# A mixed four-stage transformer block on one core: products over the full array that nothing reads, in the first stretch of the heads stage

## What is computed

```python
x = L0_attn_embedding                              # (4, 1024, 128)
x = _layernorm(x + _L0_attn_ref(x, Wq, bq, ...))   # 16 heads of 8
x = _layernorm(x + _L0_ffn_ref(x, ...))            # 2 layers of local attention and a gated ffn
x = _layernorm(x + _L1_attn_ref(x, ...))           # rotary positions, Taylor softmax
x = _layernorm(x + _L1_ffn_ref(x, ...))

# _L0_attn_ref
q, k, v = split_heads(e @ Wq + bq), split_heads(e @ Wk + bk), split_heads(e @ Wv + bv)
scores = jnp.einsum('bhqd,bhkd->bhqk', q, k) * scale
attn = jax.nn.softmax(scores, axis=-1)
av = jnp.einsum('bhqk,bhkd->bhqd', attn, v)
out = av.transpose(0, 2, 1, 3).reshape(b, s, e) @ Wo + bo
```

## Time and profile before

| | us |
|---|---|
| median of 3 runs | 1731.61 |
| the runs | 1735.49, 1728.04, 1731.61 |
| the profiled execution, its own time | 1729.86 |
| span of its trace | 1728.1 |

### The profile page before, as it was taken

How to read it: one execution, slowest core, us unless ns; L and a number is a source line. 1 busy time by engine, 2 the same in 40 slices (tenths; PEclk the granted TensorE clock), 3 DMA queues, 4 the chain that set the end, 5 groups by cost and what they waited for, 6 DMA issues and landing times. The chain is left out here.

```text
span 1728.1 us, 41224 instructions
## 1 busy us (share of the span) xinstructions
PE 1574.9 (91%) x14986; PEld 806.7 (47%) x14986; DVE 1393.2 (81%) x2949; ACT 1187.2 (69%) x2461; POOL 787.9 (46%) x605
## 2 busy tenths in 40 slices
PE   6499999999999999968999998999999989699887
PEld 4122223223223232244777775667777755344454
DVE  6799999999999999646999996689999968343355
ACT  5168888888888888865788784267888744555421
POOL 4211111112221114247888882288888825644301
PEclk9589999999999999988999999999999999999999
DMA  5203111000000000111223222322232222000001
GB/s 166 75 20 129 34 36 38 20 20 20 21 20 20 21 22 17 49 51 39 59 57 83 61 54 62 80 53 62 57 92 62 55 57 66 1 1 2 1 18 32
DMA packets 124384, 79.14 MB, mean 46 GB/s; under 512 B 50594, under 2 KB 110940, under 8 KB 123932
## 3 DMA queue, kind: packets, MB, share of 16 engines
q1 hardware_dynamic: 122796, 75.44, 16.4%
q10 hardware_dynamic: 1392, 1.12, 0.2%
HBM read 42.82 MB, written 16.79 MB: 34 GB/s over the span
## 5 line engine op out<-in xcount | busy, mean ns | idle before, releaser
L1101 DVE TENSOR_REDUCE hd_top<-hd_pX 128x1 f32<-128x512 f32 x1024 | 623.6, 680 | 32.8 <-PE hd_pX L935 32.8
L1069 ACT ACTIVATE hd_E<-hd_pS 128x1024 f32<-128x1024 f32 x512 | 524.7, 1025 | 82.1 <-PE hd_pS L951 59.9
L935 PE MATMUL hd_pX<-l_K,l_Q 48*128 48x512 bf16 x1024 | 342.3, 396 | 26.1 <-DMA l_Q<-q_parts 21.5
L968 PE MATMUL hd_pO<-hd_E,l_V 128*32 128x256 f32 x4096 | 327.6, 392 | 18.0 <-ACT hd_O L1044 18.0
L951 PE MATMUL hd_pS<-l_Q,l_K 50*128 50x512 bf16 x1024 | 310.5, 384 | 3.0 <-DMA l_Q<-hd_negp 2.0
L883 POOL TENSOR_TENSOR hd_inv<-hd_OS,hd_minus 128x16 f32<-128x16 f32 x31 | 90.0, 2902 | 443.4 <-ACT hd_OS L1057 430.8
L1815 POOL TENSOR_TENSOR w_inv<-w_ss,w_mhalf 128x16 f32<-128x16 f32 x64 | 186.4, 2913 | 0.0
L1710 ACT ACTIVATE w_pS<-w_pS,w_nb 128x128 f32<-128x128 f32 x512 | 178.5, 365 | 6.5 <-DVE w_nb L1901 4.7
L1804 POOL TENSOR_TENSOR w_C<-w_C,w_N 128x1024 f32<-128x1024 f32 x64 | 151.0, 2360 | 61.3 <-DVE w_N L1875 61.0
L968 PEld LDWEIGHTS hd_pO<-hd_E,l_V 128*32 128x32 f32 x4096 | 81.7, 108 | 171.3 <-issue 124.7
L951 PEld LDWEIGHTS hd_pS<-l_Q,l_K 50*128 50x128 bf16 x1024 | 59.0, 94 | 197.8 <-issue 184.7
(11 more groups left out here) (290 smaller groups left out, 2785.0 us busy)
## 6 DMA issues: line engine op xcount, KB each, us to landing
w_VA<-w_V SPq DMA_DIRECT2D x127, 128.0 KB, 2.3
l_Q<-q_parts SPq DMA_DIRECT2D x192, 32.0 KB
l_K<-k_parts SPq DMA_DIRECT2D x168, 32.0 KB
m<-early_rows SPq DMA_DIRECT2D x64, 64.0 KB, 1.7
f_H<-m SPq DMA_DIRECT2D x32, 128.0 KB, 2.7
f_X<-m SPq DMA_DIRECT2D x16, 256.0 KB, 3.0
q_parts<-pj_ptq SPq DMA_DIRECT2D x8, 384.0 KB, 2.5
k_parts<-pj_ptk SPq DMA_DIRECT2D x8, 384.0 KB, 2.5
```

The source lines that it names most:

```text
L935: nc.tensor.matmul(px[:, :], Q[m.j][rows, m.z, b, t * P:(t + 1) * P], K[m.j][rows, b, k * 512:(k + 1) * 512], start=True, stop=True).then_ ...
L968: last = nc.tensor.matmul(pO[VW * b:VW * b + VW, cols], V[n.j][:, b * NT + g, :], E[g % SLOTS][:, b, cols], start=(g == 0 and half == 0), ...
L1069: nc.scalar.activation(E[g % SLOTS][:, 2 * k:2 * k + 2, :], pS[k][:, :, :], ACT.Exp).then_inc(exped[k], 1)
L1101: nc.vector.tensor_reduce(top2[m.z][:, ROW_ORDER[q], k:k + 1], pX[slot][:, :], AX.X, ALU.max).then_inc(topped, 1)
```

## The change

TensorE gets two kinds of products whose results are never read. `idle_rows`: a float32 product of 128 rows by 128 columns with 512 columns streamed, out of `v_all` into `pO`; five of them stand ahead of the first product of maxima, and so ahead of its wait for the operands. `idle_keys`: a bfloat16 product of 128 rows by 128 columns with 256 columns streamed, out of the first head's K into half of `pO` (unit 0) or of `pS[0]` (unit 1); one stands behind each of the 44 products of maxima of the loop. Since `pS[0]` takes the first turned rotary rows, TensorE waits ahead of unit 1 until ScalarE has copied them. Nothing is removed, and the other engines' instructions stay as they are.

```diff
@@ -979,10 +979,24 @@
                     last.then_inc(o_turned, 1)
                     turned[1] = n
 
+                def idle_rows():
+
+                    nc.tensor.matmul(pO[:, :], v_all[:, 0, :], v_all[:, 0:CT, :].rearrange("p t d -> p (t d)"), start=True, stop=True)
+
+                def idle_keys(m):
+
+                    bank = pO if m.n == 0 else pS[0][:, 0, :]
+                    nc.tensor.matmul(bank[:, 0:2 * P], K[0][:, 0, 0:P], K[0][:, 0, 0:2 * P], start=True, stop=True)
+
+                for _ in range(5):
+                    idle_rows()
                 for m, rows in ((Unit(0), ROWS), (Unit(1), AHEAD - ROWS)):
+                    if m.n == 1:
+                        pe.wait_ge(kept.rope_taken, 1)
                     for q in range(rows):
                         for k in range(2):
                             cross(m, q, k)
+                            idle_keys(m)
                         if m.n == 0 and q >= ROWS - 8 and q % 2:
                             n = (q - ROWS + 8) // 2
                             kept.turn_rows(pe, n // 2, n % 2, pS[n // 2][:, n % 2, :])
```

## The result

The changed kernel takes 1741.12 us (median of 6 runs, 1739.78 to 1741.99); the kernel before, measured beside it, 1730.19 (6 runs, 1725.88 to 1735.49). The ratio is 1.006 with a 95% interval of 1.004 to 1.008: slower by 10.9 us. That is over the half per cent that the prediction took as its bound, though the interval's lower end is not; that the kernel is slower is clear. The profiled execution has a span of 1740.2 us, 12.1 more than before's.

The account below looks back on a forecast made before the run. VectorE bounds the stretch before, TensorE after: first 20 pairs +6.0, three turns +4.4, last 12 pairs +4.0, less the exchange's shift, +13.7; early high-clock pairs make it +13.1. Added to 1731.6: 1744.7 us, range 1732 to 1750.

Parts of the forecast that it names:

- The five products ahead: TensorE before the first operands land: five products from about 53.2 to 58.7-61.8 us, hidden by the loading, costing nothing.
- The sign: Named as wrong: a first product of maxima later than 64 us, which would mean the five products are not hidden.
- The high clock is lost before it is of use: TensorE around the operands' landing: high clock lost between 61 and 66 us, after some 4 us of idling.
- The filler does not lift it: Maxima up to the scores: a 256-column product behind each product of maxima leaves the clock low, as before.
- The pair: Product of maxima plus filler on TensorE: 0.887 us at the low clock against VectorE's 0.598; 0.515 at the high clock.
- VectorE's holes: VectorE during the maxima, 66 to 80 us: holes of 0.29 us each, released by TensorE.
- The sum: Delay at the first score: +13.7 us at the low clock, +13.1 with half the saving of four high-clock pairs.
- The way from turn to turn: Between turns of rotary rows, three times: 4.46 us instead of 2.98, +1.48 each, +4.4 together.
- The exchange: Unit 0's negated maxima, split on GpSimd and turned by TensorE: start at 96.1 us, +9.7, after the fourth turn's +10.4.
- All of it reaches the end: From the first product at 63.62 us: whatever is lost or won before 102 us reaches the kernel's end in full.
- the clock that stays high: Rival: high clock from the five products to the scores, VectorE paces all; -3.1 us, 1728.5 us; chance 0.16.
- The switch that is free: Rival: low clock, no cost between array shapes, a pair takes 0.640 us; +3 us, 1734.6 us; chance 0.08.

Follow-up runs that it names:

- rows_only: Changed kernel with the five products ahead kept and the products between the maxima left out; 1731.77 us, ratio to before 1.0004.
- keys_48rows: Changed kernel with each product between the maxima on the same 48 rows as the product of maxima ahead of it, in other banks; 1730.70 us, ratio to before 0.9997.
- keys_128cols: Changed kernel with 128 instead of 256 columns in each product between the maxima; 1737.67 us, ratio to before 1.0041.
- rows9_keys: Changed kernel with nine products ahead of the operands instead of five; 1740.34 us, ratio to before 1.0057.
- keys_only: Changed kernel without the five products ahead, the products between the maxima kept; 1742.22 us, ratio to before 1.0073.
- hold_even: Against before: eleven float32 products ahead, 256 float32 columns behind every second product of maxima except before rotary turns, long ones at negated maxima and first scores; 1727.76 us, ratio 0.9982.

## Why the prediction was right, step by step

- **The five products ahead.** Forecast to run from 53.2 to between 58.7 and 61.8 and to cost nothing: 53.20 to 60.73, and rows_only has no difference that can be told. A first product of maxima later than 64 was named as a sign of being wrong, and it stood at 64.46. TensorE had idled 3.73 us by then, so the products were hidden all the same; the operands landed later, which with the same five products they did not in keys_48rows (63.75). The sign was badly chosen.
- **The high clock is lost before it is of use.** Forecast between 61 and 66: it was 1.00 in 64 to 66 and 0.54 in 66 to 67. The outcome was right; the reason given, some 4 us of idling, is possible but not shown for this kernel. Here the clock outlived the 3.73 us of idling and fell 1.6 us into the pairs, 5.3 us after the last of the five products. In rows_only and keys_128cols, with the same five, it fell during the idling, 3.7 and 3.8 us after the last of them, so idling alone is enough. In rows9_keys it fell 4 us into the pairs with 0.54 us of idling, so the pairs are enough too. Which of the two did it in the changed kernel these runs do not separate.
- **The filler does not lift it.** 0.50 from 67 to 117 us, as forecast, and in keys_only from 53 us on.
- **The pair.** Forecast 0.887 at the low clock, measured 0.867: the way into the full array is 0.107 as read (66.06 to 66.60 less 0.427), the way back is 0.12 instead of 0.14 (66.60 to 66.93 less 0.213). The 0.14 was taken from behind four float32 transposes. VectorE's holes, forecast at 0.29, are 0.17 in its records, for the reason given above; the spacing of 0.87 is what counts. At the high clock 0.515 was forecast and 0.533 measured, still under VectorE's 0.598.
- **The sum.** Forecast 13.7, less 0.6 for a few pairs at the high clock. In the trace it is 41.55 - 29.73 = 11.8. The difference of 1.3 is in the sizes of its terms. The 32 pairs outside the turns were 0.02 us shorter, 0.6 together. The way from turn to turn was 4.31 (80.66 to 84.97) instead of 4.46, 0.4 for the three. The pairs at the high clock saved 1.0 instead of 0.6. The exchange took 0.1 more (93.61 to 95.31). The first score was forecast near 106.5 and stood at 106.01, closer than the sum deserves, because the operands landed 0.84 us later. The range, 1732 to 1750, held; the point, 1744.7, was 3.6 us high, of which 1.4 is the median of before that it was added to (1731.61, then 1730.19 beside the changed kernel) and 1.3 the sum; the rest is within the scatter of the runs.
- **All of it reaches the end.** The delay in the trace is 12.7 us at the first score (0.8 of it the later landing), 13.6 at the second fold (the low clock lasts 11 us behind the first score, 9 before), 12.3 at the fifth, 12.9 at the last of the heads stage and 12.1 at the end. The step down by 1.3 is one wait for a DMA, on TensorE's timeline of the kernel before and then of the changed one:

```profile
157.61 0.39 PE L951 MATMUL hd_pS<-l_Q,l_K 50*128 50x512 bf16 x1 [1.54 <-DMA l_Q<-hd_negp]
```

```profile
169.93 0.39 PE L951 MATMUL hd_pS<-l_Q,l_K 50*128 50x512 bf16 x1 [0.24 <-DMA l_Q<-hd_negp]
```

  SyncE issues these stores behind the loads of the later stages' weights; that this delays them is not shown. From the fourth fold to the fifth the ten traces show 20.4 to 23.0 us in no order by kernel, so this is scatter and not a part of the change.
- **The rivals.** Of the clock that stays high, the forecast was a gain of 3.1 us. hold_even brings that state about in another way, and from first product to second fold its trace shows 3.4 (44.86 - 41.42); 1.4 of them go to its late start. At the last fold of the stage it is 3.3 ahead, of which 1.3 come later and mostly from the wait of the fifth fold (20.79 us behind the fourth, 21.84 before), which is scatter. The switch that is free is out: the pair took 0.867 us and not 0.640, and keys_48rows and keys_128cols say why. The same rows bound the gap between products that the Trainium skill gives ("TensorE: Matmul & The Clock Gate", "Back-to-back issue gap"; columns over the clock, at the low one). It holds between products of one shape (74.59 to 75.02 in keys_48rows is 0.43 for 512 columns) and misses 0.11 us at each change of shape.

## What to carry to other kernels

An instruction that nobody reads is not free when the engine it fills is not far ahead of the one that sets the pace: price it with what it does to its neighbours (here two changes of the array's shape, 0.23 us, more than its own 0.21 us of columns), and at the clock at which it will run if it fails to raise it. Before trying to hold a clock, work out what holding it is worth from the holes in the pacing engine's timeline: here some 3 us of 1730, against 11 to lose. What held it here was full-array float32 work, spread evenly with few changes of shape and no gap at the handover; which of these matters was not separated. One long product in four did it, by the mean clocks, only in some runs.

## What the runs showed of the hardware

- Going from a product on 48 rows to one on 128 rows and back costs 0.11 and 0.12 us at 1.2 GHz and 0.21 together at 2.4 GHz; it hardly follows the clock. Between products of one shape it is nothing, also where one of them is unread (0.43 us for 512 columns in keys_48rows). What the array does in that time no run shows.
- The high clock outlived 3.73 us in which TensorE did nothing, and fell later, when TensorE's records covered every microsecond (66 to 67 us in the changed kernel, near 67.9 with nine products ahead). With the same five products in rows_only it fell during the idling, 3.7 us after the last one. A TensorE that looks busy in the records can lose its clock, and one that idles can still have it.
- The first product of maxima, where it waited for its operands, stood between 63.62 and 64.46 us in eight traces, and with the same five products ahead between 63.75 and 64.46.
